# Shorter lags in the MLP stage: a change of the software pipeline in a four-layer convolution kernel

## The chip, the cores and the metric

The kernel runs on one core of a Trainium2 chip. Its five engines take their instructions from queues of their own and in order: TensorE (PE; the trace shows its weight loads apart, as PEld), VectorE (DVE), ScalarE (ACT), GpSimd (POOL) and SyncE (SP, which issues all DMAs here). The metric is the device time of one execution in microseconds (us), lower is better. Times in the text count from the start of the span of the profiled execution, unless a step is laid out from zero, which is said there.

## The reference, cut to what matters

Four layers run one after the other on an input of 4 images, 128 channels, 96x96: a split into low and high frequencies with 1x1 convolutions (L0), a selective-scan block (L1), an attention block with an MLP (L2), and a binary 3x3 convolution (L3). The change touches the end of L2 alone:

```python
t = shortcut + ta * act_res @ outproj_w + outproj_b
t = t + img2tok(_dwconv(tok2img(t), cpe2_w, cpe2_b))     # 3x3, one filter per channel
tn2 = _ln(t, n2_g, n2_b)                                 # mean and variance over the 128 channels
mlp = gelu(tn2 @ fc1_w + fc1_b) @ fc2_w + fc2_b          # 128 -> 512 -> 128
t = t + mlp                                              # its sign is what L3 convolves
```

## The kernel before

**Tiles and stages.** Channels lie on the 128 partitions. An image is cut into NB = 12 blocks of 8 rows (128x768, fp32; a product on TensorE is made in two halves of 384 columns, because a PSUM bank holds no more than 512). For every image `middle(i)` runs stage after stage, and in each stage every engine has a list of (lag, stage function) pairs, given to `pipelined`: in step t an engine calls the functions of its list in the order of the list, each for block t - lag. The order of the work on an engine is thus written out by hand; between engines only semaphores count (`done(i, b)` is the value a semaphore has when block b is finished). All but the first and last steps run inside a hardware loop, two steps per turn.

**The MLP stage** (called g in the code) has these parts for a block b:

- ScalarE makes the centre tap (`first_tap`, L855) and two side taps (`term`, L876), each a 128x768 pass. POOL adds the side taps (`add_term`, L696, two adds per block).
- VectorE adds four more taps (`chain_tap`, L240), then `tap_7` (L1600) and `tap_8` (L1605). This gives t.
- TensorE multiplies t by a centring matrix into PSUM banks 2 and 3 (`g_centre`, L1243); ScalarE squares it (`g_squares`, L966); TensorE averages the squares into banks 6 and 7 (`g_variance`, L1248); ScalarE takes Ln (L971) and Exp (L973) of it (`g_root`, L968, which first loads the table set for them, L969); VectorE multiplies (`g_normalise`, L1611). This is the layer norm.
- TensorE makes the four quarters of fc1 (`up(0)` to `up(3)`, L1253), ScalarE the Gelu of each (`gelu(j)`, L978), TensorE the four parts of fc2 (`down(0)` to `down(3)`, L1261), which add up in banks 4 and 5. VectorE adds the result to t (`x3`, L1615), and ScalarE takes the sign (`sign`, L983).

**What holds the order.** All four `up` products write the same two banks, 0 and 1: `up(j)` waits until the Gelu of the product before it has read them. Banks 2 and 3 hold the centred values until `g_normalise` has read them, and the next `g_centre` waits for that. TensorE's products are recorded as L1027, from the helper `product`, and `down` as L1267. In the step order of before, TensorE's list is up(0), down(3) of the block before, up(1), down(0), up(2), down(1), variance, up(3), down(2), centre; ScalarE's is gelu(0), centre tap, sign, gelu(1), two terms, gelu(2), root, gelu(3), squares.

Of the kernel before, what the change touches and what calls it, by code (L numbers as in the profile page):

```python
# [52 lines left out]
def pipelined(eng, count, stages):  # L53

    deepest = max(lag for lag, _ in stages)

    def step(t, parity, whole):  # L60
        for lag, stage in stages:
            if whole or 0 <= t - lag < count:
                stage(t - lag, (parity - lag) % 2)

    start = min(deepest + 1, count)
    pairs = (count - 1 - start) // 2
    for t in range(start):
        step(t, t % 2, False)
    if pairs >= 2:
        with eng.Fori(0, pairs, 1) as k:  # L70
            for u in range(2):
                step(2 * k + (start + u), (start + u) % 2, True)
        start += 2 * pairs
    for t in range(start, count + deepest):
        step(t, t % 2, False)
# [25 lines left out]
def build(nc, t, out):  # L101

    B, _, S, _ = t["x"].shape
    NB = S // ROWS
# [12 lines left out]
    def done(i, b):  # L117

        return i * NB + (b + (1 + CREDIT))

    def steps(i, b, each, step):

        return i * (NB * each) + (b * each + step)
# [6 lines left out]
    with ctx:  # L130
# [8 lines left out]
        def pair(bank):  # L139

            return psum[:, bank:bank + 2, 0:HC]
# [21 lines left out]
        def tile(n):  # L163
            return work[:, n * BLK:(n + 1) * BLK]
# [4 lines left out]
        def halves(ap):  # L169
            return ap.rearrange("p (a c) -> p a c", a=2)  # L170
# [58 lines left out]
        def col(name, n=0, rows=slice(0, P)):  # L229
            return cols[rows, at[name] + n:at[name] + n + 1]  # L230
# [4 lines left out]
        def chain_tap(eng, i, conv, n, k, tile_of):  # L235

            def stage(b, p):
                tgt = by_row(tile_of(p))
                eng.wait_ge(tap_done[n - 1], tapped(i, b))
                eng.scalar_tensor_tensor(out=tgt, in0=prow(k, b, *TAPS[n]), scalar=tap_weight(conv, TAPS[n]), in1=tgt,  # L240
                                         op0=ALU.mult, op1=ALU.add).then_inc(tap_done[n], 1)
            return stage

        def chain_tile(conv, n, p):

            return region_tile(0, 2 * n + p)
# [496 lines left out]
        def _(a):  # L743
# [39 lines left out]
            def middle(i):  # L783
# [75 lines left out]
                def terms(conv, k, lag, rows, used):  # L859

                    def free(b):
                        a.wait_ge(tap_done[1], tapped(i, b - 2))
                        a.wait_ge(rows, done(i, following(b)))

                    return [(lag, first_tap(conv, k, lambda p: chain_tile(conv, 0, p), free))] +\
                        [(lag, term(conv, n, k, used)) for n in TERM_TAPS]
# [108 lines left out]
                def gelu(j):  # L975
                    def stage(b, p):
                        a.wait_ge(g_fc1, steps(i, b, 4, 4 * CREDIT + j + 1))
                        a.activation(halves(tile(4 + j)), pair(0), ACT.Gelu, bias=col("fc1_o", j)).then_inc(g_gelu, 1)  # L978
                    return stage

                def sign(b, p):
# [3 lines left out]

                all_done(a, i, f2_lepe, f2_ta)
                tap, first, second = terms("cpe2", 1, 0, f2_t2, g_t)
                pipelined(a, NB, [(4, gelu(0)), tap, (6, sign), (4, gelu(1)), first, second, (4, gelu(2)), (3, g_root),
                                  (4, gelu(3)), (2, g_squares)])

            a.wait_ge(borders, 1)
            pipelined(a, NB, [(3, silu_z(0)), (0, relus(0))])
            with a.Fori(0, B - 1, 1) as i:
                middle(i)
                a.wait_ge(borders, i * 5 + 6)
                pipelined(a, NB, [(3, silu_z(i + 1)), (0, relus(i + 1)), (0, scale_out(i, lambda p: 5))])
            middle(B - 1)
            pipelined(a, NB, [(0, scale_out(B - 1, lambda p: 5 * p))])

        @block.tensor
        def _(pe):
# [20 lines left out]
            def product(bank, terms):  # L1023

                for s in range(2):
                    for n, (weights, moving) in enumerate(terms):
                        last = pe.matmul(psum[:, bank + s, 0:HC], weights[:, :], moving(s),  # L1027
                                         start=(n == 0), stop=(n == len(terms) - 1))
                return last

            def flat_rows(k, b):
                return lambda s: R[k][:, ds(BLK * b + HC * s, HC)]
# [4 lines left out]
            def static(ap):  # L1037
                return lambda s: ap[:, HC * s:HC * (s + 1)]
# [42 lines left out]
            def middle(i):  # L1081
# [171 lines left out]
                def up(j):  # L1253
                    def stage(b, p):
                        if j == 0:
                            pe.wait_ge(g_tn, done(i, b))
                        pe.wait_ge(g_gelu, steps(i, b, 4, 4 * CREDIT + j))
                        product(0, [(fc1[:, P * j:P * (j + 1)], flat_rows(2, b))]).then_inc(g_fc1, 1)
                    return stage

                def down(j):  # L1261
                    def stage(b, p):
                        if j == 0:
                            pe.wait_ge(g_x3, done(i, b - 1))
                        pe.wait_ge(g_gelu, steps(i, b, 4, 4 * CREDIT + j + 1))
                        for s in range(2):
                            last = pe.matmul(psum[:, 4 + s, 0:HC], fc2[:, P * j:P * (j + 1)], static(tile(4 + j))(s),  # L1267
                                             start=(j == 0), stop=(j == 3))
                        if j == 3:
                            last.then_inc(g_fc2, 1)  # L1270
                    return stage

                pipelined(pe, NB, [(4, up(0)), (5, down(3)), (4, up(1)), (4, down(0)), (4, up(2)), (4, down(1)),
                                   (3, g_variance), (4, up(3)), (4, down(2)), (2, g_centre)])

            pipelined(pe, NB, [(3, xz(0)), (0, l0(0))])
            with pe.Fori(0, B - 1, 1) as i:
                middle(i)
                all_done(pe, i, g_x3)  # L1280
                pe.wait_ge(borders, i * 5 + 5)
                pipelined(pe, NB, [(3, xz(i + 1)), (0, l0(i + 1)), (0, l3(i, lambda p: 5, 1))])
            middle(B - 1)
            all_done(pe, B - 1, g_x3)
            pe.wait_ge(borders, (B - 1) * 5 + 5)
# [4 lines left out]
        def _(v):  # L1290
# [118 lines left out]
            def middle(i):  # L1409
# [203 lines left out]
                def x3(b, p):  # L1613
# [2 lines left out]
                                           in1=halves(flat(3, b)), op0=ALU.add, op1=ALU.add).then_inc(g_x3, 1)  # L1616

                taps = [chain_tap(v, i, "cpe2", tap, 1, lambda p: chain_tile("cpe2", 2, p)) for tap in VECTOR_TAPS]
                pipelined(v, NB, [(1, taps[0]), (1, taps[1]), (5, x3), (1, taps[2]), (1, taps[3]), (1, tap_7), (1, tap_8),
                                  (3, g_normalise)])  # L1620

            begin(0, False)
            with v.Fori(0, B - 1, 1) as i:
                middle(i)
                begin(i + 1, True)
            middle(B - 1)

# [85 lines left out]
```

## Time and profile before

| what | value |
|---|---|
| time, median of 3 runs | 3776.42 us (3766.5 to 3781.95) |
| time of the profiled execution | 3766.47 us |
| its span, first to last instruction | 3764.7 us |
| PE busy | 2961.8 us (79%) |
| DVE busy | 2484.8 us (66%) |
| ACT busy | 2364.5 us (63%) |
| POOL busy | 1088.9 us (29%) |
| mean granted TensorE clock | 0.926 |

Busy shares are means over stages with different limits, so they say little on one stage. In a timeline a row is: start, length, engine, line, operation, result<-operands, shape, how many instructions were merged into the row, and in brackets the idle time ahead of it with what ended it.
### The profile page before, as it was taken

How to read it: one execution, taken by the hardware profiler on the slowest of the kernel's cores; microseconds unless marked ns; L12 is line 12 of the kernel's file. 1: busy time of each engine (PE TensorE's matmuls, PEld its weight loads, DVE VectorE, ACT ScalarE, POOL GpSimd, SP SyncE). 2: the span in 40 equal slices, each digit the busy share in tenths (PEclk: the TensorE clock that was granted, in tenths of full speed). 3: DMA queues.
4: the chain of work that ended last, by engine and by line, in shares of the span. 5: the costliest groups of instructions: out<-in, count | busy, mean ns of one | idle time of the engine just before them, and what ended most of it. 6: DMA issues, size and time to landing. Idle time of an engine off the chain costs nothing.

```text
span 3764.7 us, 53610 instructions
## 1 busy us (share of the span) xinstructions
PE 2961.8 (79%) x17500; PEld 1601.7 (43%) x17500; DVE 2484.8 (66%) x2565; ACT 2364.5 (63%) x2677; POOL 1088.9 (29%) x612
## 2 busy tenths in 40 slices
PE   3688876969968877787995887776998788858699
PEld 2344335435534434444552433443554344344355
DVE  5687556865568645687466964768635786476771
ACT  2787535467679744446778864543868876454484
POOL 0235102632034500363103530146210352025530
PEclk9899988989989999898998999988999999988899
DMA  2001463600200147340020034743002004465101
GB/s 69 13 1 39 117 186 113 163 9 0 76 18 0 39 125 216 109 129 9 0 88 5 0 81 113 203 131 90 9 11 82 0 0 130 122 175 141 50 0 50
DMA packets 137194, 274.36 MB, mean 73 GB/s; under 512 B 17139, under 2 KB 93622, under 8 KB 137014
## 3 DMA queue, kind: packets, MB, share of 16 engines
q1 hardware_dynamic: 137014, 272.01, 26.1%
q8 instruction: 107, 1.75, 0.2%
q14 instruction: 73, 0.60, 0.1%
HBM read 194.07 MB, written 77.88 MB: 72 GB/s over the span
## 4 chain that ended last, share of the span: by engine, by line
PE 49%; DVE 24%; issue 11%; ACT 9%; DMA 4%; POOL 1%; SPq 1%; DVEq 1%; ACTq 0%; POOLq 0%
PE psum L1027 31%; PE psum L1267 5%; PE psum L1047 5%; DVE work L1444 4%; DVE work L1417 4%; PE psum L1075 3%; DVE region L1544 2%; DVE psum L1435 2%; DVE region L240 2%; DVE work L1429 2%; DMA work<-scratch_dwc 2%; PE psum L1225 2%; PE psum L1226 1%; DVE region L1611 1%; ACT work L971 1%
## 5 line engine op out<-in xcount | busy, mean ns | idle before, releaser
L1498 DVE SCALAR_TENSOR_TENSOR work<-region,cols,work 128x768 f32<-128x768 f32 x288 | 392.3, 1362 | 15.1 <-DVE work L1498 7.5
L696 POOL TENSOR_TENSOR region<-region 128x768 f32<-128x768 f32 x96 | 211.1, 2203 | 370.9 <-ACT region L876 365.2
L1027 PE MATMUL psum<-region,m_cen 128*128 128x384 f32 (+1 forms) x384 | 162.8, 550 | 168.5 <-DVE region L1611 62.3
L1027 PE MATMUL psum<-region,m_fc 128*128 128x384 f32 (+1 forms) x768 | 282.8, 491 | 10.8 <-ACT work L978 10.8
L1267 PE MATMUL psum<-work,m_fc 128*128 128x384 f32 x768 | 282.5, 491 | 0.0
L660 POOL TENSOR_TENSOR work<-work 128x768 f32<-128x768 f32 x48 | 113.9, 2376 | 503.4 <-ACT work L796 416.9
L1417 DVE SCALAR_TENSOR_TENSOR work<-region,cols,work 128x768 f32<-128x768 f32 x144 | 202.2, 1430 | 78.0 <-POOL work L660 61.9
L1027 PE MATMUL psum<-work,m_avg 128*128 128x384 f32 x576 | 224.2, 514 | 15.1 <-ACT work L838 7.2
L672 POOL TENSOR_TENSOR work<-work,region 128x768 f32<-128x768 f32 x96 | 174.5, 1817 | 211.6 <-DVE work L1429 211.6
L240 DVE SCALAR_TENSOR_TENSOR region<-region,cols 128x768 f32<-128x768 f32 x192 | 223.8, 1165 | 17.9 <-POOL region L696 9.9
L978 ACT ACTIVATE work<-psum,cols 128x768 f32<-128x768 f32 x192 | 173.1, 901 | 88.2 <-PE psum L1027 85.2
L710 POOL COPY region<-work 128x768 f32<-128x768 f32 x4 | 3.3, 828 | 711.4 <-DVE work L1535 711.4
L1027 PEld LDWEIGHTS psum<-region,m_fc 128*128 128x128 f32 x768 | 144.2, 192 | 121.3 <-ACT work L978 40.0
L1267 PEld LDWEIGHTS psum<-work,m_fc 128*128 128x128 f32 x768 | 142.1, 190 | 111.5 <-DVE region L1615 21.2
L942 ACT ACTIVATE region<-psum,cols 128x768 f32<-128x768 f32 x48 | 43.2, 901 | 231.6 <-PE psum L1027 231.6
L1027 PEld LDWEIGHTS psum<-region,m_cen 128*128 128x128 f32 x384 | 70.4, 204 | 261.4 <-issue 129.5
L1027 PE MATMUL psum<-region,m_dwl 128*128 128x384 f32 (+1 forms) x192 | 91.7, 562 | 103.2 <-DVE work L1417 103.2
L1027 PE MATMUL psum<-region,m_w_dt 128*128 (+1 forms) x384 | 145.0, 503 | 23.0 <-DVE work L1429 12.7
L1444 DVE TENSOR_TENSOR_SCAN work<-work,psum 128x768 f32<-128x768 f32 x88 | 159.6, 1814 | 3.1
L1027 PEld LDWEIGHTS psum<-work,m_avg 128*128 128x128 f32 x576 | 110.5, 198 | 111.5 <-ACT work L838 27.6
L1047 PE MATMUL psum<-work,m_dwc_shifted 64*32 64x384 f32 x2304 | 119.6, 549 | 47.6 <-DMA work<-scratch_dwc 47.6
L1615 DVE SCALAR_TENSOR_TENSOR region<-psum,cols,region 128x768 f32<-128x768 f32 (+1 forms) x48 | 48.8, 1018 | 159.7 <-PE psum L1267 159.7
(234 smaller groups left out, 7548.7 us busy)
## 6 DMA issues: line engine op xcount, KB each, us to landing
work<-scratch_cpe SPq DMA_DIRECT2D x192, 196.0 KB, 4.1
work<-scratch_dwc SPq DMA_DIRECT2D x192, 196.0 KB, 4.1
work<-scratch_lepe SPq DMA_DIRECT2D x192, 196.0 KB, 3.9
region<-in_tab_ch SPq DMA_DIRECT2D x48, 768.0 KB, 5.2
region<-in_x SPq DMA_DIRECT2D x48, 384.0 KB, 3.3
region<-in_tab_tok SPq DMA_DIRECT2D x48, 384.0 KB, 3.1
out<-work SPq DMA_DIRECT2D x48, 384.0 KB, 2.3
scratch_cpe<-region SPq DMA_DIRECT2D x44, 392.0 KB, 4.6
```

Source lines behind the costliest of these rows:

```text
L240: eng.scalar_tensor_tensor(out=tgt, in0=prow(k, b, *TAPS[n]), scalar=tap_weight(conv, TAPS[n]), in1=tgt, op0=ALU.mult, op1=ALU.add).then_i ...
L660: g.tensor_tensor(tile(4 + p), tile(p), tile(2 + p), ALU.add).then_inc(b_taps[0], 1)
L672: g.tensor_tensor(tile(2 + p), tile(p), flat(2, sweep_block(sweep, b)), ALU.mult).then_inc(c["du"], 1)
L696: g.tensor_tensor(chain_tile(conv, n, p), chain_tile(conv, n - 1, p), chain_tile(conv, n, p), ALU.add).then_inc(tap_done[n], 1)
L978: a.activation(halves(tile(4 + j)), pair(0), ACT.Gelu, bias=col("fc1_o", j)).then_inc(g_gelu, 1)
L1027: last = pe.matmul(psum[:, bank + s, 0:HC], weights[:, :], moving(s), start=(n == 0), stop=(n == len(terms) - 1))
L1047: last = pe.matmul(psum[32 * j:32 * j + 32, bank + s, 0:HC], shifted[conv][half, c0:c0 + 32], rows[half, j, :, dw:dw + S], start=(fresh an ...
L1075: last = pe.matmul(psum[:, bank(p) + s, 0:HC], w3[:, P * k:P * (k + 1)], signs()[:, ds(ROWS * b + (1 + dh + HALF * s), HALF), 1 + dw:1 + d ...
L1267: last = pe.matmul(psum[:, 4 + s, 0:HC], fc2[:, P * j:P * (j + 1)], static(tile(4 + j))(s), start=(j == 0), stop=(j == 3))
L1417: v.scalar_tensor_tensor(out=by_row(tile(6 + p)) if n == 4 else sofar, in0=prow(3, b, *scan_tap(n)), scalar=col("l1taps", n), in1=sofar, o ...
L1444: v.tensor_tensor_scan(way(tile(6 + p)), way(tile(4 + p)), way(bu_flat), initial=start, op0=ALU.mult, op1=ALU.add).then_inc(c["h"], 1)
L1498: v.scalar_tensor_tensor(out=by_row(tile(acc + p)), in0=prow(k, b, *TAPS[n]), scalar=tap_weight(conv, TAPS[n]), in1=by_row(tile(acc + p)), ...
```

## The change

Three lists of (lag, function) pairs get new lags and a new order. No function, wait, tile or semaphore is changed. The lags of the fc products and Gelus go from 4 to 3 (`down(3)` from 5 to 4), of `x3` from 5 to 4, of `sign` from 6 to 5. The centring product and the squares go from lag 2 to 1, the step of the block's taps. The variance and the root go from lag 3 to 2 and are called earlier in the step: the variance ahead of `up(2)` and no longer after `down(1)`, the root after `gelu(1)` and ahead of the two terms, no longer after `gelu(2)`. The normalisation goes from lag 3 to 2 and from the end of VectorE's step to ahead of `tap_7` and `tap_8`.

```diff
@@ ScalarE
-                pipelined(a, NB, [(4, gelu(0)), tap, (6, sign), (4, gelu(1)), first, second, (4, gelu(2)), (3, g_root),
-                                  (4, gelu(3)), (2, g_squares)])
+                pipelined(a, NB, [(3, gelu(0)), tap, (5, sign), (3, gelu(1)), (2, g_root), first, second, (3, gelu(2)),
+                                  (3, gelu(3)), (1, g_squares)])
@@ TensorE
-                pipelined(pe, NB, [(4, up(0)), (5, down(3)), (4, up(1)), (4, down(0)), (4, up(2)), (4, down(1)),
-                                   (3, g_variance), (4, up(3)), (4, down(2)), (2, g_centre)])
+                pipelined(pe, NB, [(3, up(0)), (4, down(3)), (3, up(1)), (3, down(0)), (2, g_variance), (3, up(2)), (3, down(1)),
+                                   (3, up(3)), (3, down(2)), (1, g_centre)])
@@ VectorE
-                pipelined(v, NB, [(1, taps[0]), (1, taps[1]), (5, x3), (1, taps[2]), (1, taps[3]), (1, tap_7), (1, tap_8),
-                                  (3, g_normalise)])
+                pipelined(v, NB, [(1, taps[0]), (1, taps[1]), (4, x3), (1, taps[2]), (1, taps[3]), (2, g_normalise), (1, tap_7),
+                                  (1, tap_8)])
```

## Rows read from the trace of the kernel before

**Rows 1.** The page, the chain of work that ended last, by engine.

```profile
PE 49%; DVE 24%; issue 11%; ACT 9%; DMA 4%; POOL 1%; SPq 1%; DVEq 1%; ACTq 0%; POOLq 0%
```

**Rows 2.** Busy time by stretch, first image: us, PE, PEld, DVE, ACT, POOL, clock.

```profile
796.48:810.83 14.35, 12.59 (x38) 6.91 (x37) 5.69 (x7) 12.57 (x13) 3.62 (x2) 0.97 0.10 28
810.83:921.18 110.35, 106.41 (x322) 59.00 (x321) 76.96 (x63) 92.90 (x100) 32.56 (x18) 1.00 0.01 4
921.18:934.77 13.59, 13.23 (x42) 7.38 (x41) 1.97 (x2) 9.46 (x10) 0.00 (x0) 1.00 0.00 0
934.77:948.13 13.36, 11.86 (x38) 6.51 (x36) 1.97 (x2) 9.46 (x10) 0.00 (x0) 1.00 0.00 1
```

**Rows 3.** Timeline of TensorE in one full step: up(0), variance, centre.

```profile
810.83 1.45 PE L1027 MATMUL psum<-region,m_fc 128*128 128x384 f32 x4
...
818.65 1.45 PE L1027 MATMUL psum<-work,m_avg 128*128 128x384 f32 x4
...
823.05 1.53 PE L1027 MATMUL psum<-region,m_cen 128*128 128x384 f32 x4 [0.37 <-DVE region L1611]
```

**Rows 4.** Timeline of ScalarE in the same step.

```profile
812.32 0.90 ACT L978 ACTIVATE work<-psum,cols 128x768 f32<-128x768 f32 x1 [0.48 <-PE psum L1027]
...
814.90 0.90 ACT L978 ACTIVATE work<-psum,cols 128x768 f32<-128x768 f32 x1 [0.76 <-PE psum L1027]
815.70 1.75 ACT L876 ACTIVATE region<-region,cols 128x768 f32<-128x768 f32 x2
...
818.48 1.28 ACT L969 ACT_TABLE_LOAD   x1
820.14 0.90 ACT L971 ACTIVATE work<-psum,cols 128x768 f32<-128x768 f32 x1 [0.38 <-PE psum L1027]
821.08 0.84 ACT L973 ACTIVATE work<-work 128x768 f32<-128x768 f32 x1
821.94 1.28 ACT L978 ACT_TABLE_LOAD   x1
```

**Rows 5.** Timeline of VectorE in the same step: tap_8 beside a POOL add.

```profile
817.69 2.45 DVE L1605 SCALAR_TENSOR_TENSOR region<-region,cols 128x768 f32<-128x768 f32 x1
```

**Rows 6.** Timeline, a Gelu and the up product that waits for it.

```profile
947.17 0.90 ACT L978 ACTIVATE work<-psum,cols 128x768 f32<-128x768 f32 x1
...
948.13 1.56 PE L1027 MATMUL psum<-region,m_fc 128*128 128x384 f32 x4 [1.50 <-ACT work L978]
```

**Rows 7.** Timeline of POOL, VectorE, TensorE and ScalarE as the stage fills.

```profile
761.66 10.49 POOL L696 TENSOR_TENSOR region<-region 128x768 f32<-128x768 f32 x5 [2.09 <-ACT region L876]
...
765.46 8.55 DVE L240 SCALAR_TENSOR_TENSOR region<-region,cols 128x768 f32<-128x768 f32 x4 [1.97 <-POOL region L696]
...
776.04 5.60 DVE L240 SCALAR_TENSOR_TENSOR region<-region,cols 128x768 f32<-128x768 f32 x4
...
792.70 0.95 DVE L1611 TENSOR_TENSOR region<-work,psum 128x768 f32<-128x768 f32 x1
...
776.17 2.93 PE L1027 MATMUL psum<-region,m_cen 128*128 128x384 f32 x4 [13.86 <-DVE region L1605]
...
793.79 2.90 PE L1027 MATMUL psum<-region,m_cen 128*128 128x384 f32 x4 [10.86 <-DVE region L1611]
...
779.14 0.81 ACT L966 ACTIVATE work<-psum 128x768 f32<-128x768 f32 x1 [2.05 <-PE psum L1027]
```

**Rows 8.** Timeline of TensorE elsewhere: one wait twice, in two images.

```profile
393.66 1.98 PE L1027 MATMUL psum<-region,m_w_l1out 128*128 128x384 f32 x4 [2.37 <-POOL region L688]
395.56 3.38 PE L1047 MATMUL psum<-work,m_cpe_shifted 64*32 64x384 f32 x48
...
3157.33 1.56 PE L1027 MATMUL psum<-region,m_w_l1out 128*128 128x384 f32 x4 [2.37 <-POOL region L688]
3158.82 2.17 PE L1047 MATMUL psum<-work,m_cpe_shifted 64*32 64x384 f32 x48
```

**Rows 9.** Busy time by stretch and granted clock right after those two waits.

```profile
394.70:398.10 3.40, 3.40 (x34) 0.88 (x40) 2.39 (x4) 2.27 (x3) 1.67 (x8) 0.50 0.02 5
...
3157.40:3160.00 2.60, 2.60 (x36) 1.25 (x44) 1.07 (x3) 2.59 (x3) 0.98 (x8) 1.00 0.02 6
```

## The prediction, made before the changed kernel ran

> **What bounds the kernel now.** I read the chain of work that ended last first: TensorE carries half of it [rows 1], so a stage in which TensorE is dense is paid in full. The change is confined to one stage, so next I cut the MLP stage of the first image into its steps. A step is one block's four up and four down products, one variance and one centring product. Eight full steps take 110.35 us, 13.79 us each, and TensorE is busy for 106.41 of that; ScalarE is busy for 92.90, VectorE for 76.96 [rows 2]. Inside one step, the six products from up(0) at 810.83 to the variance at 818.65 come 1.30 us apart, and the one wait of TensorE is 0.37 us, for the normalisation ahead of the centring product [rows 3]. Ten products at 1.29 make 12.9 of the 13.6 us. So the stage is bound by TensorE, ScalarE has under 3 us to spare per step, and what is to be seen in ScalarE's rows is where its work lies between the four Gelus: the two terms (1.75) between gelu(1) and gelu(2), the root with a table load on both sides between gelu(2) and gelu(3) [rows 4]. The ups share one pair of PSUM banks, so each up waits for the Gelu before it, and each such gap on ScalarE must fit between two ups.
>
> **The change, part by part.** The instructions are the same in number and kind; all that moves is order.
>
> *Root ahead of the terms.* I lay out a step from zero at up(0), products 1.29 apart, with the new list. An up's Gelu starts 1.49 after the up (812.32 after 810.83 [rows 3, 4]), and an up that waits for a Gelu starts 0.96 after that Gelu's start (948.13 after 947.17 [rows 6]). up(0) 0, gelu(0) 1.49, down(3) 1.29, up(1) 2.58 (its Gelu condition is met at 2.45), gelu(1) 4.07 to 4.97, down(0) 3.87, variance 5.16, up(2) 6.45, down(1) 7.74 to 9.03. ScalarE meanwhile: table load 4.98 to 6.26; Ln waits for the variance until 5.16 + 1.49 = 6.65 (818.65 to 820.14 is the same 1.49 [rows 3, 4]); Exp 7.59 to 8.45; then the two terms, 1.78 with their issue, to 10.23; then the Gelu table load, 1.29, to 11.52; only now gelu(2), whose up(2) has been ready since 7.9. So up(3) starts at 11.52 + 0.96 = 12.48, where TensorE was free for it at 9.03. Before, up(3) could follow the variance without a wait. The rest of the step is up(3), down(2), centre: 12.48 + 3 x 1.29 = 16.35, with the two small pauses of 0.08 seen before 16.5. The steps inside the loop took 0.4 more than those outside before (eight steps average 13.79, one alone is 13.59 [rows 2]); I add 0.2. A full step is 16.7 in place of 13.79: eight of them +23.2 us per image.
>
> Which steps are full follows from the lags: the terms run for block t until t = 11, the fc products for block t - 3, so blocks 0 to 8 have terms beside them. Block 9 has the root but no terms: gelu(2) at 8.45 + 1.29 = 9.74, up(3) 10.70, step 14.7 in place of 13.59 [rows 2]: +1.1. Block 10 has no centring product: 10.70 + 2 x 1.29 = 13.3 and a small pause, against 13.36 [rows 2]: nothing. Block 11 has neither root nor variance: nothing.
>
> *Centring in the step of the taps; normalisation ahead of tap_7.* In a full step these cost nothing while the stall of up(3) covers them. Normalisation runs from 8.5 to 9.4 and frees the centring banks long before the centring product at 15.1, so the old wait of 0.37 is gone. tap_7 and tap_8 follow it on VectorE, beside both POOL adds, since the terms now end at 10.2; such an instruction took 2.45 [rows 5], so t is ready at about 14.3, 0.8 ahead of the centring product that waits for it. If that cover were gone, the price is what t is late beyond 15.1, under 1 us in a step. x3 waits for down(3) at 1.29 + 1.49 = 2.8 as before, and the four plain taps of the next block start when the second POOL add is through, at about 14.5. SP and POOL get nothing moved past them.
>
> *Fill.* Squares(0) now stands ahead of block 2's taps on ScalarE and waits for the centring product, so of POOL's five adds in a row, 10.49 us [rows 7], the fifth comes later. The four taps of block 0 took 8.55 beside them and the next four 5.60 beside one add [rows 7]; I take 1.9 off, so t(0) is ready at 774.2 and centre(0) starts 774.3 (was 776.17 [rows 7]). At the low clock of this stretch a product's reader starts 2.97 after it (776.17 to 779.14 [rows 7]): squares 777.3 to 778.1, tap to 779.1, load to 780.4, Ln at 778.1 + 2.97 = 781.1, Exp to 782.9, normalisation to 783.8. VectorE has waited for this 4.6 us with tap_7 and tap_8 of block 1 behind it, which then end at 787.3 (one of them beside an add, 2.45). centre(1) takes 2.7, and up(0) of block 0 starts at 790.0 instead of 796.48 [rows 2, 7], because the normalisation of block 0 no longer stands behind block 2's taps (792.70 [rows 7]). That is -6.5 us per image: the gain of the shorter pipeline. The first fc step then costs more: up(0) at the low clock, gelu(0) behind a table load at 792.9, up(1) 793.9 at the low clock, gelu(1) 796.8 to 797.7, load to 799.0, Ln at 800.1, Exp to 801.9, terms, load to 805.0, up(3) 806.0, up(0) of block 1 at 809.8: 19.8 us, against 14.35 [rows 2]: +5.4.
>
> *TensorE's clock.* Each full step now has a gap in TensorE's work of 9.2 to 12.5, some 3.3 us; before, the stage had none over 1 us in its full steps and its clock stood at 1.00 [rows 2]. What follows such a gap is to be read elsewhere in the trace. The same wait of 2.37 us stands in two images: in one the granted clock then fell to 0.50 (1.2 GHz) from 394.7 to 398.1, in the other it stayed at 1.00 [rows 8, 9]. The work after it took 393.66 to 398.94 = 5.28 us in the first and 3157.33 to 3160.99 = 3.66 in the second: 1.6 us lost [rows 8]. Everything that TensorE does in the 8 us after the gap (up(3), down(2), centre, up(0) to the variance) is on the path to the next root, so the loss counts in full. A gap of 3.3 us is longer than one that does it at times; I take a loss in each of the nine full steps, 1.7 each, 15.3 per image; bounds 0 (never, as in the second image) and 3.3 (the low clock held twice as long).
>
> *Sum per image:* -6.5 + 5.4 + 23.2 + 1.1 = +23.2, with the clock +38.5. Four images alike: +93 or +154. Against the profiled execution, 3766.5: 3859 without the clock, 3920 with it. That execution lies 10 us under the median of the runs; I don't add the 10, since the spread of the runs is 15.
>
> Two rules of the Trainium skill bear on this. The rows show a table load of 1.28 us and the Ln 0.38 after its end, for which the row names TensorE [rows 4]. The Trainium skill (ScalarE: Activation LUTs, on what ACT_TABLE_LOAD costs) adds a drain of about 1380 ns to each switch of table sets; both switches now lie between gelu(1) and gelu(2), so by the page each full step would be an estimated 2.8 us longer still, some 3960 or more in all; the rows leave no room for it. Of the clock, the rows show it halved after a gap of 2.37 us once and not another time [rows 8, 9]. The Trainium skill (TensorE: Matmul & The Clock Gate, the section on HAM oscillation) puts as its rule that only idle gaps longer than the one forecast here halve the clock; by the page the result is the 3859 of the rival below, and the first of the two rows speaks against it.
>
> **The rivals.** *The clock holds:* the same stall, but TensorE stays at 2.4 GHz, as after one of the two waits [rows 8, 9]: 3859. Against it: the gap is 0.9 us longer than those. *The clock stays low twice as long in each step:* 3.3 in place of 1.7: +58 more, 3978. *The other side, faster:* the gap on ScalarE between gelu(1) and gelu(2) is hidden, and what is left is the gain of the fill, -6.5, and of the centring wait, some 0.4 to 0.5 in ten steps: -11 per image, 3722. It decides at 9.03 us: gelu(2) would have to start by 8.1 after up(0), where I have 11.52; both table loads (2.57) would have to vanish and nearly 1 us more. I see nothing in the rows for it but that the ends of matmuls are modelled. *No visible change:* the stall is real but ScalarE runs so far ahead that half of it is hidden; against it, ScalarE can't run ahead of an up, since each Gelu waits for its own.
>
> **How the numbers follow.** Stall with clock loss in most steps 0.57, stall without it 0.22, clock low twice as long (or the drain of the page) 0.13, hidden and faster 0.04, hidden in part and the same 0.04. The likeliest gives 3920. The range reaches down to the case without clock loss, less 14 for its own errors (0.4 us in a full step is 14 us), and up to 3965, three quarters of the way to the doubled loss: 3845 to 3965. About 0.5% is what a measurement of this kernel tells from no change: faster 0.04, same 0.04, slower 0.92.
>
> **What would show it.** Right: in a full step, up(3) with an idle time of about 3.3 us ahead of it, released by a Gelu; gelu(2) right behind a table load; ScalarE no longer waiting for up(2); starts of up(0) 16.7 us apart, or some 18.4 with a stretch at clock 0.50 behind the gap; up(0) of block 0 about 30 us after the stage's first tap at 759.7, not 36.8; no wait of the centring product for the normalisation. Wrong: steps of 14 us or less, or up(3) starting without a wait. Whatever t is late by would show as a wait of the centring product for L1605.

## The result, and the profile after

| | before | after |
|---|---|---|
| median | 3779.18 us (3766.5 to 3784.18, 4 runs, one more than in the table of before) | 3928.53 us (3919.65 to 3935.8, 4 runs) |
| ratio, 95% interval | | 1.0399 (1.0362 to 1.0437) |
| span of the profiled execution | 3764.7 us | 3920.7 us |
| mean granted TensorE clock | 0.926 | 0.913 |

The change makes the kernel 4.0% slower. The forecast was 3920 us, 154 more than the profiled execution of before; the median is 3928.5, 149 more than the median of before.

The stretches of the first image in the kernel after, cut at the starts of up(0) as those of before were. The columns are those of [rows 2]: us, busy time of PE, PEld, DVE, ACT and POOL, granted clock, share and GB/s of the DMAs.

```profile
796.63:815.48 18.85, 13.92 (x37) 7.46 (x36) 9.40 (x8) 12.57 (x13) 4.89 (x2) 0.91 0.08 21
815.48:962.70 147.22, 122.02 (x321) 66.51 (x320) 84.38 (x64) 95.45 (x103) 33.85 (x16) 0.88 0.01 3
...
849.90:861.00 11.10, 9.40 (x29) 4.99 (x27) 5.65 (x6) 9.73 (x11) 1.44 (x1) 1.00 0.01 1
861.70:868.30 6.60, 5.85 (x9) 3.20 (x10) 4.71 (x4) 1.60 (x2) 2.14 (x1) 0.50 0.00 0
882.20:885.40 3.20, 3.20 (x6) 1.69 (x6) 3.03 (x3) 0.61 (x1) 1.14 (x1) 0.50 0.00 0
```

The first two rows answer to the first two of [rows 2]: the step of block 0 takes 18.85 us in place of 14.35, and eight full steps 147.22 in place of 110.35, 18.4 each. The mean clock of the eight steps is 0.88 in place of 1.00: within a step it is 1.00 until the gap and, in seven of the eight, 0.50 behind it, sometimes for about 3 us and sometimes for over 6. The last three rows show it: the step from 849.89 ahead of its gap, the low stretch behind that gap, and the one behind the next.

The timeline of TensorE in one full step of after, from up(0) at 849.89 to the next up(0) at 869.39:

```profile
849.89 1.45 PE L1027 MATMUL psum<-region,m_fc 128*128 x4
...
855.27 1.45 PE L1027 MATMUL psum<-work,m_avg 128*128 128x384 f32 x4
...
857.85 1.45 PE L1267 MATMUL psum<-work,m_fc 128*128 128x384 f32 x4
862.45 2.93 PE L1027 MATMUL psum<-region,m_fc 128*128 x4 [3.15 <-ACT work L978]
865.17 2.77 PE L1267 MATMUL psum<-work,m_fc 128*128 128x384 f32 x4
867.73 1.82 PE L1027 MATMUL psum<-region,m_cen 128*128 x4
869.39 1.45 PE L1027 MATMUL psum<-region,m_fc 128*128 x4
```

up(3) at 862.45 has waited 3.15 us for a Gelu; up(3) and down(2) then take 2.7 and 2.6 us from start to start, at the low clock, where a product takes 1.29 at the full one. The centring product at 867.73 has no wait any more: in [rows 3] it was the only product with one.

The timeline of ScalarE in the same step, which answers to [rows 4]:

```profile
853.96 0.90 ACT L978 ACTIVATE work<-psum,cols 128x768 f32<-128x768 f32 x1
854.88 1.28 ACT L969 ACT_TABLE_LOAD   x1
856.76 0.90 ACT L971 ACTIVATE work<-psum,cols 128x768 f32<-128x768 f32 x1 [0.59 <-PE psum L1027]
857.69 0.84 ACT L973 ACTIVATE work<-work 128x768 f32<-128x768 f32 x1
858.44 1.75 ACT L876 ACTIVATE region<-region,cols 128x768 f32 x2
860.20 1.28 ACT L978 ACT_TABLE_LOAD   x1
861.50 0.90 ACT L978 ACTIVATE work<-psum,cols 128x768 f32<-128x768 f32 x1
865.42 0.90 ACT L978 ACTIVATE work<-psum,cols 128x768 f32<-128x768 f32 x1 [3.02 <-PE psum L1027]
```

From the start of gelu(1) to the start of gelu(2) ScalarE has 7.54 us of work without a pause but 0.59, and up(2) had been ready since 858 (it started at 856.56). All of it stands between two ups that share their banks.

### The profile page after: what moved, and what is told of

It reads as the page before. It is cut to its first block and busy times, and to the rows that moved or that the text cites. A ratio compares the mean times of both kernels' runs of the same rounds, so it can differ in the third digit from the quotient of the medians.

```text
span 3920.7 us, 53768 instructions
## 1 busy us (share of the span) xinstructions
PE 3033.0 (77%) x17500; PEld 1635.3 (42%) x17500; DVE 2497.4 (64%) x2565; ACT 2362.4 (60%) x2677; POOL 1084.1 (28%) x612
## 5 line engine op out<-in xcount | busy, mean ns | idle before, releaser
L1027 PE MATMUL psum<-region,m_fc 128*128 128x384 f32 (+1 forms) x768 | 327.9, 555 | 130.1 <-ACT work L978 130.1
L1498 DVE SCALAR_TENSOR_TENSOR work<-region,cols,work 128x768 f32<-128x768 f32 x288 | 391.9, 1361 | 15.1 <-DVE work L1498 6.7
L1267 PE MATMUL psum<-work,m_fc 128*128 128x384 f32 x768 | 308.1, 528 | 0.0
L1027 PEld LDWEIGHTS psum<-region,m_fc 128*128 128x128 f32 x768 | 155.3, 212 | 264.6 <-ACT work L978 177.1
L240 DVE SCALAR_TENSOR_TENSOR region<-region,cols 128x768 f32<-128x768 f32 x192 | 206.6, 1076 | 41.9 <-POOL region L696 32.0
L1027 PE MATMUL psum<-work,m_avg 128*128 128x384 f32 x576 | 220.5, 506 | 15.1 <-ACT work L838 7.2
L1267 PEld LDWEIGHTS psum<-work,m_fc 128*128 128x128 f32 x768 | 156.9, 209 | 130.7 <-issue 32.4
L1615 DVE SCALAR_TENSOR_TENSOR region<-psum,cols,region 128x768 f32<-128x768 f32 (+1 forms) x48 | 48.9, 1018 | 243.1 <-PE psum L1267 243.1
L1027 PEld LDWEIGHTS psum<-region,m_cen 128*128 128x128 f32 x384 | 78.4, 217 | 212.9 <-issue 99.7
```

The costliest lines, as they stand in the source:

```text
L1498: v.scalar_tensor_tensor(out=by_row(tile(acc + p)), in0=prow(k, b, *TAPS[n]), scalar=tap_weight(conv, TAPS[n]), in1=by_row(tile(acc + p)), ...
L1615: v.scalar_tensor_tensor(out=halves(flat(3, b)), in0=pair(4), scalar=col("fc2_b"), in1=halves(flat(3, b)), op0=ALU.add, op1=ALU.add).then_ ...
```

## The experiments

Each kernel is compared with runs of the kernel before on the same chip, whose median was 3773.0 to 3774.4 us there, and 3779.2 beside the kernel after. So a comparison of two changed kernels takes for each its distance from its own before. Times are medians; ratios are to the kernel before, with the 95% interval. "The stage" is the time from the first tap of the MLP stage to its last x3, read from the traces; added up over the four images it is 802.0 us before and 946.1 after.

**lags_only: the lags without the new order.** On top of the change, the order inside the step as before:

```diff
-  ACT  (3, gelu(1)), (2, g_root), first, second, (3, gelu(2)), (3, gelu(3))
+  ACT  (3, gelu(1)), first, second, (3, gelu(2)), (2, g_root), (3, gelu(3))
-  PE   (3, down(0)), (2, g_variance), (3, up(2)), (3, down(1)), (3, up(3))
+  PE   (3, down(0)), (3, up(2)), (3, down(1)), (2, g_variance), (3, up(3))
-  DVE  (1, taps[3]), (2, g_normalise), (1, tap_7), (1, tap_8)
+  DVE  (1, taps[3]), (1, tap_7), (1, tap_8), (2, g_normalise)
```

> The shorter lags of the change with the old places in the step: the variance after down(1), the root after gelu(2), the normalisation at the end of VectorE's step. Theory (the stall comes from the place of the root, not from the lags): up(3) starts without a wait, full steps are 13.6 to 14.0 us again, the fill of each image is 6 to 8 us shorter than before; 3779 - 4 x 6.5 = about 3753 us. Rival (the lags are too short for the chain of layer norm, so the centring product or up(0) waits in every step whatever the order): 3779 or more, with waits of the centring product for L1605 or of up(0) for L1611.

Measured: 3747.32 us (3740.24 to 3749.02), ratio 0.9929 (0.9905 to 0.9953). The shorter lags alone are a gain of 26 us, small but clear of the spread. Who made TensorE wait in the first image's stage (waited for, total us, times, longest), two rows of lags_only, then one of the kernel before and one of the kernel after:

```profile
PE psum L1027 <- DVE region L1611: 10.2, 11, 5.2
PE psum L1027 <- ACT work L978: 3.2, 2, 1.7
...
PE psum L1027 <- DVE region L1611: 15.5, 11, 10.9
...
PE psum L1027 <- ACT work L978: 33.1, 12, 3.2
```

The Gelu is in it for 3.2 us in two waits, the first and the last block's, as before; in the kernel after it is 33.1 us in 12 waits. The waits for the normalisation (L1611) are ten short ones, 5.0 us in all (4.6 before), and one while the stage fills, which is 5.2 in place of 10.9. The lags aren't too short for the layer norm's chain.

**order_only: the new order with the old lags.** The three lists of the change with every lag of the kernel before.

> The old lags with the new places in the step (root after gelu(1) ahead of the terms, variance ahead of up(2), normalisation ahead of tap_7). Theory: the same stall of up(3), 3.15 us, in every full step, a low clock behind it, and the long fill of before: the changed kernel's 3928 plus what its shorter fill gave, 4 x 6 = 24: about 3950 us. Rival (the stall needs the short lags): about 3779 us.

Measured: 3925.66 us (3918.57 to 3932.75), ratio 1.0412 (1.0384 to 1.0439). The order alone makes the whole loss: 153 us here, 149 with the shorter lags. TensorE's waits in the first image:

```profile
PE psum L1027 <- ACT work L978: 31.4, 12, 3.2
```

But it came out 24 us below the expectation, level with the kernel after. With the new order the shorter lags gain nothing that the spread of the runs would show: up(0) of block 0 starts 34.8 us after the stage's first tap (794.87 after 760.03) where it was 30.8 in the kernel after (796.63 after 765.88). But terms run for blocks up to 11 and the fc products for block t - 4, so only the blocks 0 to 7 have terms beside their fc products, where lag 3 gives nine. A step with terms takes over 18 us here and one without them 14.8, so most of the 4 us won in the fill are lost again. I had counted the nine steps for the forecast and forgotten them for this expectation.

**root_back: only the root back behind gelu(2).**

```diff
-                (3, gelu(1)), (2, g_root), first, second, (3, gelu(2)),
+                (3, gelu(1)), first, second, (3, gelu(2)), (2, g_root),
```

> The changed kernel with only the root put back behind gelu(2) on ScalarE; variance and normalisation stay where the change put them. Theory: up(3) no longer waits, but Exp ends at about 11.9 us of the step, the normalisation at 12.9, and tap_7 and tap_8 stand behind it on VectorE, so the centring product waits for L1605 until about 15.1 in place of 11.6: a gap of 3.5 us in another place, steps of 16.4 plus the clock loss, 3900 to 3950 us. Rival (the place of the root on ScalarE is all of it): steps of 13.6, 3750 to 3780 us.

Measured: 3929.25 us (3925.61 to 3930.96), ratio 1.0412 (1.0389 to 1.0435): no better than the change. TensorE and VectorE in one of its steps:

```profile
879.24 1.45 PE L1267 MATMUL psum<-work,m_fc 128*128 128x384 f32 x4
884.26 1.55 PE L1027 MATMUL psum<-region,m_cen 128*128 x4 [3.57 <-DVE region L1605]
...
881.01 0.95 DVE L1611 TENSOR_TENSOR region<-work,psum 128x768 f32 x1 [6.29 <-ACT work L973]
881.88 1.01 DVE L1600 SCALAR_TENSOR_TENSOR region<-region,cols 128x768 f32<-128x768 f32 x1
883.08 1.02 DVE L1605 SCALAR_TENSOR_TENSOR region<-region,cols 128x768 f32 x1 [0.18 <-DVE region L1600]
```

The gap is as long, 3.57 us, but sits ahead of the centring product: VectorE waited 6.29 us for Exp with tap_7 and tap_8 queued behind the normalisation, and centring at lag 1 needs tap_8. An early normalisation in front of tap_7 needs an early root; the three lists hang together.

**filled_gap: the clock by itself.** Two centring products whose result nobody reads, in the gap ahead of up(3). The edit adds four lines, so that the normalisation is L1615 in this kernel and down L1271:

```diff
+                        if j == 3 and not (isinstance(b, int) and b > 8):
+                            pe.wait_ge(g_tn, done(i, b + 1))
+                            for _ in range(2):
+                                product(2, [(cen128, flat_rows(3, b))])
                         pe.wait_ge(g_gelu, steps(i, b, 4, 4 * CREDIT + j))
```

> The changed kernel with two more centring products, whose result nobody reads, on TensorE in the gap ahead of up(3), blocks 0 to 8 and all in the loop; they wait for the normalisation, start near 9.5 us of the step and end near 12.2, before up(3) can start at 12.5. Theory (the idle stretch makes the clock fall): the granted clock stays 1.00 in the full steps, these are 16.5 us in place of 18.4 on average, up(3) still starts 0.96 after the start of gelu(2); 3928 - 4 x 15 = about 3868 us. Rival (the clock falls for another reason, or the low clock costs nothing on the path): 3928 or more.

Measured: 3854.04 us (3851.93 to 3857.74), ratio 1.0214 (1.0191 to 1.0236), 81 us above its before where the kernel after is 149 above its own: 68 us better with more work on TensorE. The eight full steps of the first image, one of them, and from the step ahead of that one the rows of TensorE and ScalarE around the gap (the two extra products are the row with x8; L1615 is the normalisation):

```profile
807.00:939.02 132.02, 128.66 (x386) 70.56 (x385) 84.65 (x65) 95.45 (x103) 33.94 (x16) 1.00 0.01 4
...
839.94:856.45 16.51, 16.07 (x49) 8.82 (x48) 10.71 (x9) 12.02 (x13) 4.15 (x2) 1.00 0.00 1
...
833.29 2.82 PE L1027 MATMUL psum<-region,m_cen 128*128 x8 [0.48 <-DVE region L1615]
835.97 1.56 PE L1027 MATMUL psum<-region,m_fc 128*128 x4
...
835.01 0.90 ACT L978 ACTIVATE work<-psum,cols 128x768 f32<-128x768 f32 x1
```

A step is 16.5 us, the clock 1.00 in all eight, and up(3) still starts 0.96 us after gelu(2). The stage takes 877.4 us in all four images: 75 more than before with the clock held, and the kernel after takes 69 more than that. So of the loss in the stage about half is the stall and about half the low clock behind it. It came out 14 us below the expectation of 3868, which was counted from the median of 3928, measured beside a before of 3779 and not of 3773, with 60 us for the clock.

**terms_late: the two terms out of the interval.**

```diff
-                (3, gelu(1)), (2, g_root), first, second, (3, gelu(2)),
+                (3, gelu(1)), (2, g_root), (3, gelu(2)), first, second,
```

> The changed kernel with the two terms behind gelu(2) and no longer between the root and gelu(2). Theory: gelu(2) at 9.74 us of the step, up(3) at 10.70, a gap of 1.5 us, after which the clock doesn't fall as a rule; full steps 14.7 to 14.9, about 3795 us (3785 to 3815). Rival (only the two table loads around the root matter, the terms would find another wait): above 3850 us.

Measured: 3796.24 us (3793.17 to 3799.41), ratio 1.0057 (1.0039 to 1.0076). One step, and the wait in it:

```profile
841.90:856.93 15.03, 13.43 (x41) 7.38 (x40) 7.81 (x8) 12.02 (x13) 3.62 (x3) 1.00 0.01 1
...
852.96 1.56 PE L1027 MATMUL psum<-region,m_fc 128*128 x4 [1.50 <-ACT work L978]
```

1.75 us of terms, moved by one place, are worth 127 us of the 149 (22 are left over its before): they take the gap from 3.15 to 1.50, and the clock is 1.00 in every step behind the first, in all four images.

**one_table: the gap shortened by a table load.** This kernel leaves out the Gelu, so its result isn't the reference's; it is of use for its times alone.

```diff
-                        a.activation(halves(tile(4 + j)), pair(0), ACT.Gelu, bias=col("fc1_o", j)).then_inc(g_gelu, 1)
+                        a.activation(halves(tile(4 + j)), pair(0), ACT.Identity, bias=col("fc1_o", j)).then_inc(g_gelu, 1)
```

> The changed kernel with Identity in place of Gelu, so the four activations of fc1 are no Gelu and the table load behind the root isn't needed (the one ahead of the root stays, hidden while Ln waits for the variance). Theory: gelu(2)'s place starts 1.29 us earlier, up(3) at 11.2, a gap of about 2.0 us, steps of 15.2 us at full clock: 3810 us if the clock holds, up to 3865 if it falls behind most gaps of 2.0 us. Rival (a switch of tables costs twice its row, as the Trainium skill's page ScalarE: Activation LUTs has it with a drain of 1380 ns, which no row shows here): steps shorter by 2.7 us, 3780 us or less.

Measured: 3825.68 us (3821.13 to 3827.69), ratio 1.0133 (1.0111 to 1.0156), inside the range of the theory and far from the rival. A step, cut from up(3) to the next up(3), and TensorE's waits in it:

```profile
839.66:855.99 16.33, 13.64 (x41) 7.30 (x41) 10.74 (x9) 10.63 (x12) 4.15 (x3) 1.00 0.00 1
...
839.66 1.56 PE L1027 MATMUL psum<-region,m_fc 128*128 x4 [1.72 <-ACT work L978]
...
843.47 1.55 PE L1027 MATMUL psum<-region,m_cen 128*128 x4 [0.96 <-DVE region L1605]
```

The wait of up(3) fell from 3.15 to 1.72, by 1.43 us: the load's row of 1.28 and some 0.1 of issue, not the 2.7 that it would be with the drain of the Trainium skill (ScalarE: Activation LUTs, on what ACT_TABLE_LOAD costs). But the step is 16.33 and not 15.2: a second wait, 0.96 us for tap_8, has come up that the longer stall had covered. The step of block 1, outside the loop and without that wait, took 14.98. The gaps of 1.72 and 0.96 left the clock at 1.00 in every step behind the first, in all four images, so the 3825.7 are the second wait and not the clock, which the expectation had as the only way above 3810.

**lags_var_early: a version that beats both kernels.** As lags_only, and

```diff
-                (3, up(2)), (3, down(1)), (2, g_variance), (3, up(3))
+                (3, up(2)), (2, g_variance), (3, down(1)), (3, up(3))
```

> As lags_only, with the variance one place earlier, between up(2) and down(1). Theory: Ln starts at the end of its table load in place of 0.38 us later, the normalisation ends at 11.7 us of the step, when TensorE gets to the centring product, and the wait of 0.37 to 0.62 us ahead of it goes: full steps 13.1 to 13.5 us, 3747 - 40 x 0.45 = about 3730 us. Rival (ScalarE or VectorE is then late with something else, and TensorE waits as long): 3747 us.

Measured: 3729.98 us (3724.71 to 3736.83), ratio 0.9887 (0.9866 to 0.9908), 1.1% (44 us) under the kernel before. Ln now starts right behind its table load, and in a loop step the centring product waits 0.30 us where such steps had 0.6 before (0.37 in the step of [rows 3], outside the loop). The wait shrank, it didn't go:

```profile
850.74 1.28 ACT L969 ACT_TABLE_LOAD   x1
852.04 0.90 ACT L971 ACTIVATE work<-psum,cols 128x768 f32<-128x768 f32 x1
...
855.25 1.55 PE L1027 MATMUL psum<-region,m_cen 128*128 x4 [0.30 <-DVE region L1611]
```

**var_early: that move alone, with the old lags.**

> The kernel before with the variance one place earlier, between up(2) and down(1), and the old lags. Theory (the gain of the earlier variance, 17 us in lags_var_early, and that of the shorter lags, 26 us, are separate): the wait ahead of the centring product shrinks from 0.37 to 0.62 us to under 0.3 in ten steps per image, 3774 - 17 = about 3757 us. Rival (the earlier variance helps only with the short lags): 3774 us.

Measured: 3759.38 us (3743.97 to 3761.77), ratio 0.9954 (0.9932 to 0.9976): 14 us under the kernel before on the same chip, where 17 were expected. The lags give 26, this move 14, both together 44: the two gains add up within the spread of the runs. In the first image the short waits for the normalisation shrink from 4.6 us in ten to 1.0 us in four.

## Why the prediction was right, point by point

**The ring through gelu(2) and up(3).** Right, in mechanism and size. Laid out: up(3) 12.48 after up(0), behind a gap of 3.3 us. Measured: 845.92 after 833.36 in a step at full clock, 12.56, with 3.15 of idle time:

```profile
833.36 1.45 PE L1027 MATMUL psum<-region,m_fc 128*128 x4
...
845.92 1.56 PE L1027 MATMUL psum<-region,m_fc 128*128 x4 [3.15 <-ACT work L978]
...
849.89 1.45 PE L1027 MATMUL psum<-region,m_fc 128*128 x4
```

The step is 16.53, in filled_gap 16.51; I had 16.5 and added 0.2 for the loop, which no row bears out. That the stall comes from what ScalarE has between gelu(1) and gelu(2) is shown by taking parts away: the terms (terms_late), the load (one_table), the root (root_back, where up(3) no longer waits).

**The clock.** Right in kind: filled_gap differs from the kernel after only in that TensorE is kept busy in the gap, and its clock doesn't fall. In size it was a lucky mean: 1.7 us per step were taken from one wait seen twice, with a fall behind one of the two [rows 8, 9]. Eight steps at 147.22 are 132.1 at 16.51 and 15.1 of clock, 1.9 each (13.6 were in the sum), and this mean is made of steps that lose nothing, some 1.5 or some 3.0. The rival without clock loss, +93 us, is what filled_gap shows when its condition is made true: +81. Behind the gaps of 3.15 the clock fell 31 times out of 36 in the four images, behind those of 1.50 and 1.72 in none. Of the rule in the Trainium skill (TensorE: Matmul & The Clock Gate, HAM oscillation), by which only longer gaps matter, the runs say no: 3.15 was enough.

**The table load.** The 2.8 us per step for longer switches counted both in full, though Ln waits 0.39 us for the variance anyway [rows 4] and would have hidden that much of the first; and 3960 is that on top of 3859, without the clock, so with it the case was about 4020. one_table shows that there is no such cost here: a switch taken away gave 1.43 us.

**First fc step.** Too dear. Forecast 19.8 plus a clock loss of 1.7, measured 18.85 in the first image and 17.2, 20.0 and 17.2 in the others. up(0) took 1.53 us in place of a half-clock 2.4 or more, because the clock had risen by then: the step that failed is the assumption that the low clock of the fill lasts through up(0) and up(1). [rows 2] had the answer: the same step of before, at a mean clock of 0.97. Over the four images this term is 13 us too dear, more than the 10 by which the sum exceeds the measured stage.

**Fill.** Right in direction, -6.0 against -6.5 (30.75 us from the first tap to up(0) in place of 36.76). It has the two sources that were laid out. The fifth POOL add is no longer in the row, so the first centring product starts 15.0 us after the first tap in place of 16.5; and the normalisation of block 0 no longer stands behind block 2's taps [rows 7], so the second one starts 13.0 us after the first in place of 17.6:

```profile
780.90 2.93 PE L1027 MATMUL psum<-region,m_cen 128*128 128x384 f32 x4 [12.45 <-DVE region L1605]
...
793.91 2.92 PE L1027 MATMUL psum<-region,m_cen 128*128 128x384 f32 x4 [6.26 <-DVE region L1605]
...
767.81 8.00 POOL L696 TENSOR_TENSOR region<-region 128x768 f32<-128x768 f32 x4 [2.09 <-ACT region L876]
...
771.62 7.12 DVE L240 SCALAR_TENSOR_TENSOR region<-region,cols 128x768 f32<-128x768 f32 x4 [1.99 <-POOL region L696]
...
789.50 0.95 DVE L1611 TENSOR_TENSOR region<-work,psum 128x768 f32<-128x768 f32 x1 [4.56 <-ACT work L973]
```

Four taps took 7.12 us instead of 8.55, and VectorE then waited 4.56 for Exp (I had 4.6). What I overlooked is that this gain is due to the lags and that the new order takes part of it back: in lags_only up(0) starts 28.3 us after the first tap, because there VectorE makes tap_7 and tap_8 of block 1 while it waits for Exp, and not behind the normalisation.

**Blocks 9 to 11.** Right: 14.8 us for block 9 (I had 14.7), then 13.5 for block 10, from 977.47 to 990.94 (13.36 before).

**The sum.** From first tap to last x3 the first image takes 237.0 us in place of 200.4: +36.5 where the forecast had +38.5. The other three give +33.9, +39.8 and +33.8, 144 in all against 154. The span grew by 156.0; the remaining 12 us lie in stages that the change doesn't touch. These took 2962.6 us in the profiled execution of before and 2974.6 in that of after, and between 2962 and 2979 in those of the other kernels, so they vary that much from run to run. So the hit of the total is closer than that of its terms, and that is luck: 10 us too many in the stage, 12 unforeseen outside.

**The cover of tap_8.** I wrote that the new place of the normalisation costs nothing while the stall covers it, with 0.8 us to spare. It was 0.5: in the step from 849.89 tap_8 ended 14.76 us after up(0) (I had 14.3),

```profile
862.36 2.29 DVE L1605 SCALAR_TENSOR_TENSOR region<-region,cols 128x768 f32 x1 [0.18 <-DVE region L1600]
```

and at full clock the centring product starts 15.24 us after up(0) (848.60 after 833.36). one_table took 1.43 us of the cover away and a wait of 0.96 us appeared, which is what that leaves.

## What to carry to other kernels

When a step of a software pipeline is bound by one engine, look at every pair of its products that share a buffer, and add up what the draining engine has queued between the two drains; a busy share that looks comfortable (ScalarE had 2 us to spare in a step) says nothing of that interval. Shorter lags and a new order inside the step are two changes, to be measured apart: here one gained 26 us and the other lost over 150. A stall on TensorE is to be priced with the low clock that can follow it: here the change cost 75 us in the stage with the clock held and 144 without.

## What the runs showed of the hardware that I had not expected

The low clock behind one and the same gap of 3.15 us lasted differently from step to step: the clock was 0.50 from 861.7 to 868.3 in one step (19.50 us long), from 882.2 to 885.4 in the next (18.23), and in the step from 833.37 it didn't fall at all:

```profile
833.37:849.89 16.52, 13.37 (x41) 7.38 (x40) 10.33 (x8) 12.03 (x13) 4.14 (x2) 1.00 0.02 6
849.89:869.39 19.50, 16.35 (x41) 8.82 (x40) 11.07 (x9) 12.02 (x13) 4.13 (x2) 0.82 0.00 1
869.39:887.62 18.23, 15.08 (x41) 8.20 (x40) 10.69 (x8) 12.03 (x13) 4.14 (x2) 0.91 0.00 0
```

So the loss per gap is 0, 1.7 or 3.0 us for the same gap, and a mean has to be used. Over the four images the 36 gaps had no low stretch behind them 5 times, the short one 17 times and the long one 14 times; behind the first few steps of an image the two take turns. What sets the turn is not shown here. And useless products in a gap made a kernel some 69 us faster; that is worth knowing as a test, though shortening the gap to 1.50 us (terms_late) took 124 us off the stage, and taking it away (lags_only) 174.
